# Third tile's rows and W1 ahead of the base stores in SyncE's order

## What is computed

```python
probs = softmax(flat @ gate_W)                       # 2048 rows, 8 experts
topk_w, topk_idx = top_k(probs, 2)                   # two experts a row, weights made to sum to 1
out = 0.5 * gelu(flat @ shared_W + shared_b)         # the "base" of every row
for e in range(8):
    h = gelu(flat @ W1[e] + b1[e])                   # 256 -> 1024
    out = out + combine[:, e:e+1] * (h @ W2[e] + b2[e])
out = layernorm(out) * gamma + beta                  # and x is added
```

## Time and profile before

| what | value |
|---|---|
| median of three runs | 774.73 us |
| profiled execution | 781.06 us |
| its span, first to last instruction | 779.2 us |
| PE busy | 720.6 us, 92% |
| ScalarE (ACT), VectorE (DVE), GpSimd (POOL) busy | 436.3, 378.4, 222.2 us |
| mean granted TensorE clock over the span | 0.977 |
| SyncE's store issues ahead of the third tile's rows | 502.23 to 510.19 us |
| expert stage, first transposes to last layer 2 | 502.05 to 765.85 us |

### The profile page before, as it was taken

One profiled execution on the slowest core, in us unless ns is written; L12 is line 12 of the kernel. 1 busy time (PEld: TensorE's weight loads), 2 busy tenths in 40 slices (PEclk: granted clock), 3 DMA queues, 4 the chain that ended last, 5 costly groups with the idle time before them and its releaser, 6 DMA issues.

```text
span 779.2 us, 20188 instructions
## 1 busy us (share of the span) xinstructions
PE 720.6 (92%) x7240; PEld 480.7 (62%) x7241; DVE 378.4 (49%) x1358; ACT 436.3 (56%) x772; POOL 222.2 (29%) x257
## 2 busy tenths in 40 slices
PE   4977999999999999998899898979999999999992
PEld 2434445464444444443454556778999999999991
DVE  5763221202044525348858456215665565565564
ACT  2746888988798989885557252233323333333320
POOL 2030050101000000020005135744554554554554
PEclk9999999999999999999999889999999999999997
DMA  9565958999021220304832455676666567677751
GB/s 208 147 223 185 283 144 260 275 338 319 11 84 42 65 84 22 104 3 125 264 117 75 130 176 173 197 249 212 181 220 213 187 219 249 215 226 258 232 171 57
DMA packets 91017, 135.19 MB, mean 173 GB/s; under 512 B 14558, under 2 KB 75755, under 8 KB 88602
## 3 DMA queue, kind: packets, MB, share of 16 engines
q1 hardware_dynamic: 82200, 117.71, 49.6%
q0 software_dynamic: 8736, 16.40, 6.0%
HBM read 96.13 MB, written 52.85 MB: 191 GB/s over the span
## 4 chain that ended last, share of the span: by engine, by line
PE 72%; DVE 9%; DMA 6%; ACT 6%; issue 3%; SPq 3%; POOL 1%; DVEq 0%; POOLq 0%; ACTq 0%
PE ps L2294 15%; PE ps L1951 15%; PE ps L2282 15%; PE ps L1928 13%; ACT arena L937 3%; DMA q_parts<-arena 2%; PE ps L2088 1%; DMA x_sb<-in_x 1%; PE ps L1910 1%; PE ps L1966 1%; PE ps L2004 1%; PE ps L2269 1%; SPq L616 1%; DMA k_parts<-arena 1%; PE ps L2164 1%
## 5 line engine op out<-in xcount | busy, mean ns | idle before, releaser
L937 ACT ACTIVATE arena<-ps 128x1024 f32<-128x1024 f32 x256 | 241.3, 1033 | 35.5 <-PE ps L1951 35.0
L1951 PE MATMUL ps<-arena 99*32 99x512 bf16 x2048 | 162.0, 387 | 4.4 <-issue 2.9
L1928 PE MATMUL ps<-arena 128*32 128x256 f32 x2048 | 159.6, 381 | 0.6 <-issue 0.6
L2282 PEld LDWEIGHTS ps<-arena 128*128 128x128 f32 x1120 | 130.3, 192 | 5.1 <-ACT arena L1048 1.8
L2282 PE MATMUL ps<-arena 128*128 128x128 f32 x1120 | 130.9, 275 | 2.7 <-issue 1.3
L2294 PE MATMUL ps<-arena,xh_tag 128*128 x560 | 128.0, 382 | 1.3 <-ACT xh_tag L1067 1.3
L2294 PEld LDWEIGHTS ps<-arena,xh_tag 128*128 128x128 f32 x560 | 104.8, 192 | 14.6 <-issue 1.5
L1048 ACT COPY arena<-ps 128x256 f32<-128x256 f32 x35 | 13.0, 372 | 163.6 <-PE ps L2269 158.9
L1928 PEld LDWEIGHTS ps<-arena 128*32 128x32 f32 x2048 | 65.9, 111 | 52.6 <-issue 3.4
L1951 PEld LDWEIGHTS ps<-arena 99*32 99x32 bf16 x2048 | 39.6, 95 | 71.1 <-ACT arena L937 50.0
L1067 ACT ACTIVATE xh_tag<-ps,arena 128x128 f32<-128x128 f32 x280 | 76.5, 392 | 6.8 <-PE ps L2282 6.8
(11 more groups left out here) (266 smaller groups left out, 882.2 us busy)
## 6 DMA issues: line engine op xcount, KB each, us to landing
arena<-in_L_ffn_W SPq DMA_DIRECT2D x43, 1024.0 KB, 8.8
rows_by_expert<-arena SPq DMA_DIRECT2D x9, 1965.0 KB, 15.8
arena<-q_parts SPq DMA_DIRECT2D x90, 128.0 KB, 2.6
row_parts<-arena SPq DMA_DIRECT2D x3, 2048.0 KB, 17.2
arena<-k_parts SPq DMA_DIRECT2D x42, 128.0 KB
q_parts<-arena SPq DMA_DIRECT2D x12, 384.0 KB, 2.6
arena<-rows_by_expert SPq DMA_DIRECT2D x35, 131.0 KB, 2.1
arena<-in_L_ffn_b SPq DMA_DIRECT2D x35, 128.0 KB
```

Of the source, the lines that this page charges most:

```text
L937: nc.scalar.activation(probs_of(stage, h), ps[:, 2 * (u % 2):2 * (u % 2) + 2, :].rearrange("p a n -> p (a n)"), ACT.Exp, scale=float(D) ** ...
L1928: last = nc.tensor.matmul(ps[32 * h:32 * h + 32, 4 + half, at:at + 256], v_grp[n % 2][:, kt, h, :], probs_of(stage, h)[:, 256 * part:256 * ...
L1951: last = nc.tensor.matmul(ps[c:c + 32, 2 * (u % 2) + half, :], k_stk[buf][:, h, P * st + c:P * st + c + 32], q_stk[buf][:, h, 512 * half:5 ...
L2282: last = nc.tensor.matmul(ps[:, 4 * buf + half, P * c:P * (c + 1)], w1_buf[:, buf, k, at:at + P], xs_t[:, buf, k, :], start=(k == 0), stop ...
```

## The change

SyncE issues the same DMAs in another order. The last chunk of x and the base chunk 1 now follow the load of the third tile's rows, inside start_sp; the read of its expert stands behind them, then comes its W1, and the base chunks 2 and 3 follow W1. parts_there stands after all of them, as before. Nothing changes on another engine, nor at the end of the kernel.

```diff
@@ start_sp @@
                 sp.wait_ge(xs_ps, 2 * k + 1)
                 sp.wait_ge(tag_ready, 2 * k + 1)
                 load_rows(slots_of(2 * k + 2), 0)
+                sp.wait_ge(x_last, 1)
+                store_part(3, 2, x_sb, row_out)
+                store_base(1)
+                e = expert(2 * k + 2)
                 sp.wait_ge(h_ps, 4 * k + 2)
-                load_w1(expert(2 * k + 2), 0)
+                load_w1(e, 0)
+                for ch in (2, 3):
+                    store_base(ch)
                 if k < MAYBE:
                     parts_there()
                     sp.sem_inc(may_read, 1)
@@ before begin @@
             load_w1(begin_with[1], 1)
             for j in range(2):
                 load_b2(begin_with[j], j)
-            sp.wait_ge(x_last, 1)
-            store_part(3, 2, x_sb, row_out)
-            for ch in range(1, NT // CHUNK):
-                store_base(ch)
             begin(sp, run_flags(nc.sync), start_sp)
```

## The result

The changed kernel takes 783.6 us (median of 19 runs, 779.78 to 789.07), the kernel before 779.66 us in the same comparison (19 runs, 773.8 to 786.25; the three runs of the head of this text are among them). The ratio is 1.0056, 95% interval 1.0036 to 1.0076: slower by 0.56%. The forecast was 0.9 us less than before, 773.8 us, with a range of 770.8 to 777.0; 783.6 lies outside it. On the base of the 19 runs the forecast would be 778.8 us, still 4.8 us too low, and the range 775.7 to 781.9, which leaves 783.6 outside too.

What follows compares the result with a forecast made beforehand. PE, busy 92% of the span, was taken to bound the kernel. The terms -5.1 + 0.7 + 2.2 + 1.3 = -0.9 us took the median of 774.73 us to 773.8, with a range of 770.8 to 777.0.

Steps and rivals of the forecast that it cites:

- The rest: Behind the fourth tile's layer 1: fifth tile's rows leave by 526.26 as before, jump, loop and tail unchanged; nothing added.
- -5.1: Third tile: PE's 3.30 us gap before its transposes and the half clock behind it go, 5.1 us gained.
- 0.7: Third tile's layer 1: PE newly waits 0.7 us (0 to 2.7) for its W1.
- 2.2: Fourth tile's transposes: PE newly waits 2.2 us (1.3 to 3.0) for its rows, held behind the stores' landing.
- 1.3: Fourth tile's layer 1: 1.3 us lost, between 0.9 for its W1 without a clock fall and 1.6 with one.
- Stores behind W1: Last four base stores, issued from 510.2, run until 517.2 and land at 518.2; fourth tile's rows leave at 519.7.
- a fall of the clock: Behind the fourth tile's new gap: transposes and layer 2 cost 1.3 to 1.8 us more if the clock falls.
- the jump "stays": PE's 1.31 us at the jump from the start block into the loop was to remain unchanged.
- C: Rival, slower: the wait on the stores before the fourth tile costs more than the old one, 776.8 us; chance 0.14.
- Its point of decision: Fourth tile's rows landing after 522.3 with the clock falling, after 523.9 without, make its layer 1 later than before.
- B: Rival, full gain: fourth tile's rows land before PE wants them, 5.1 us gained, 769.6 us; chance 0.08.
- The estimate from the Trainium skill: Stores' landing signal at 519.2 instead of 518.2 and all behind it 1.0 us later, a gain of about nothing.

Runs made afterwards that it cites:

- e4: Changed kernel, with base chunks 2 and 3 held back until the third tile's W1 has landed: 784.03 us (one run).
- r2: Changed kernel once more, without an edit, for a second profile: 778.81 us (one run).
- e1: Changed kernel, with SyncE's wait for the first tile's scatter moved behind the issue of the fifth tile's W1: 781.54 us, ratio 1.001 to the kernel before.
- e2: Changed kernel, with only a sixteenth of the fifth tile's W1 loaded, at the same place: 786.18 us (one run).
- r1: Kernel before once more, without an edit, for a second profile: 779.9 us (one run).
- e3: Kernel before, with the fifth tile's W1 held back until half of the fourth tile's layer 1 is done: 785.33 us (one run).
- e7: Kernel before, with SyncE waiting for the end of the fourth tile's layer 1 before it jumps into the loop: 777.61 us (one run).
- e8: Kernel before, with one more megabyte load issued by SyncE right ahead of its jump into the loop: 784.52 us (one run).
- e5: Kernel before, with the last chunk of x and base chunks 1 and 2 stored ahead of the wait for the scatters: 776.97 us, ratio 0.9952.
- e6: Kernel before, with the edits of e5 and e1 together: 776.3 us, ratio 0.9949.
- e9: Kernel before, as e6, but only the last chunk of x and base chunk 1 go ahead of the wait for the scatters: 773.71 us, ratio 0.9911.

## Why the prediction was wrong

**Two steps failed: the sizes at the third and fourth tile, and "The rest".** Of the sum, -5.1 + 0.7 + 2.2 + 1.3 = -0.9 up to the fourth layer 1 and nothing behind it, the first part came out at +1.2 and the second at +1.7 us in the two profiles of each kernel.

*The stores' landing and what it holds back.* The places were right. The third tile's rows left 2.0 us after the first transposes (forecast 504.8 - 502.05 = 2.8), PE did not wait for them, and SyncE stood in parts_there with the fourth tile's rows behind it. The sizes were not. "Stores behind W1" let the data run at 370 to 400 GB/s and end at 517.2 - 502.05 = 15.2. The last four stores were issued at 7.3, earlier than the 8.2 that I took, but from 504 to 512 the rate was 270 GB/s on average, and the data ended at 17.8. The fourth tile's rows were to leave at 519.7 - 502.05 = 17.7 and left at 18.7 to 19.5. The third W1 was taken at 6.2 us from issue to landing; it was 7.7 to 8.8 us in the four profiles with this start, at and past the upper end of the row's range, most likely because stores were issued behind it (e4). I had let only those ahead of it count. And of a fall of the clock I had counted about half; all four profiles had one before the fourth layer 1, in the third layer 1 (5.44 us) or in the second tile's layer 2 (4.94 to 6.34 us).

The gap was also compared with one profile of the kernel before, whose fourth layer 1 came at 25.4; the five profiles with that start give 23.2, 24.0, 25.4, 25.4 and 26.1, mean 24.8. The four with the changed start give 25.4, 26.1, 26.5 and 28.0, mean 26.5. So the fourth tile is 1.7 us later by these means, not 0.9 earlier; the two groups overlap, and the standard error of the 1.7 is about 0.8.

*"The rest".* The fifth tile's rows were to leave by 526.26, 24.2 us after the first transposes, because the scatter would be issued "as early as before or earlier". It was issued at 517.64 - 497.33 = 20.3 (forecast 18.5; before it was 20.0), because the stores landed late. That is nearly as before. But it landed 5.33 us later, beside the fourth tile's W1 issued 0.3 us ahead of it, instead of 2.8. The same holds in the other profiles: 5.1 to 6.1 us in changed, r2, e1, e2 and e4, where that W1 was issued 0.3 us ahead of the scatter, and 2.8 to 3.5 in before, r1, e3, e7 and e8, where it was 4.1 to 5.8 us ahead. The rows left at 27.1 (26.5 in r2). I priced the issue of a transfer and not its landing, with the new neighbour. And the sentence that the jump "stays" at 1.31 us was wrong. The late fifth load brought both on in the profiled run; e1 takes them away and gets close to the time of the kernel before (ratio 1.001). How the loss divides between them is not shown. From the fourth layer 1 to the sixth it took 16.0 and 16.3 us before, 15.9 in e1, 20.2 and 15.6 in the changed kernel.

**The sum as it was measured.** Mean of the two profiles each: 44.5 - 41.6 = 2.9 us, of which 1.2 up to the fourth layer 1 and 1.7 at the jump. The jump's part rests on one of the two profiles of the changed kernel, for r2 lost nothing there. The ratio's interval is 2.8 to 5.9 us.

**The rivals.** C (the same wait, long enough to cost more than the old gap) came closest, though about half of the loss lay at the jump, where C had nothing; that its direction was right is in that part luck. Its point of decision, the fourth rows landing past 522.3 - 502.05 = 20.3, was passed in all four profiles: they left at 18.7 to 19.5, and PE used them at 20.9 to 21.6. I gave it 0.14. B was not reached in any profile with this order of the stores, and e5 shows what it wants: most of the stores out before the stage. The estimate from the Trainium skill ("DMA: Bandwidth & Descriptors", "Anatomy of one DMA — SWDGE (gpsimd) path") on the write receipt pointed to stores landing 1.0 us later than I took, and later they were, by 1 us and more. The trace does not bear the receipt out as the cause: in the changed kernel the last packets moved at about 515.1 and SyncE's wait was over at 515.4. What came late were the data. In e4, where the four stores went alone, SyncE waited only 2.9 us for them after their last issue, against 6.3 in the changed kernel, where W1 was among them.

**The median** shown at the head came from three runs and lay 4.9 us below that of 19. That is no step of the argument, but half of the distance between the 773.8 forecast and the 783.6 measured.

## What to carry to other kernels

Before moving stores behind a load, write down every wait that counts those stores, what is queued behind the waiting instruction, and how long each transfer takes beside its new neighbours; a late wait is passed on from tile to tile until something has slack. Look for a place where the issuing engine stands idle instead (here ahead of the scatters' landing): the same stores cost 0.7 us there (1.8 us and a fall of the clock in e6) and gave back 5. Compare stretches from an event inside the stage, and take two profiles of the unchanged kernel before trusting a gap of 2 us.

## What was not expected of the hardware

- No length of a gap told whether the clock would fall: it fell to half behind 1.84 us (e6), 2.37 (e9) and 2.40 us (e2) and held behind 2.37 (e4), 2.55, 2.60 (e7) and 3.39 us (e8).
